# Cross-attention: the second half of the next tile's scores moved in among the transposes, and two probability chunks moved behind the masked copy

## The chip, the cores and the metric

The kernel runs on one core of one Trainium2 chip. Four engines compute: TensorE (PE in the profile; its weight loads are PEld), VectorE (DVE), ScalarE (ACT) and GpSimd (POOL). SyncE (SP) issues transfers. Each engine takes its instructions in order and waits on semaphores for the others. The metric is the time of one execution on the device, in microseconds (us).

## The reference

One decoder block over 2048 rows of width 256: self-attention, cross-attention onto 1601 context rows, and a layer with ternary weights. The change lies in the cross-attention:

```python
Q = q @ Wq.T + bq                     # q: layernorm(x), 2048 x 256
K = k @ Wk.T + bk                     # k, v: the context, 1601 x 256
V = v @ Wv.T + bv
e = jnp.einsum('bsd,btd->bst', Q, K) / jnp.sqrt(jnp.float32(d_k))
e = jnp.where(mask == 0, MASK_FILL, e)
a = jax.nn.softmax(e, axis=-1)
y = jnp.einsum('bst,btd->bsd', a, V)
return y @ Wo.T + bo                  # added to x
```

Everything is float32. The kernel keeps that precision by splitting an operand into a rounded high part and a low part (the difference), and multiplying the parts.

## The kernel before

The program goes through phases, each with its own block of instructions for each engine: self-attention, `fold` (it multiplies weights together so that queries meet the context directly, and values already carry the output weights), `cross`, and `feed` (the last layer). `cross` is the one that is changed. It takes the 2048 rows in 16 tiles of 128; the 1601 keys stand in 13 blocks of 128 (the last has 65), which make four `CHUNKS` of 4, 4, 4 and 1 blocks. Tiles 0 and 1 and tiles 14 and 15 are written out; tiles 2 to 13 are six turns of a hardware loop of two bodies. So there are 16 bodies, and all but the last also prepare the next tile.

For tile i, with h = i % 2 choosing the buffer:

- TensorE, `body` (L1398): `score(i+1, 0)`, the first half of the next tile's scores (12 matmuls of 512 columns into banks 0 and 1); then, once the exponentials of tile i are there (`exp_done`), the transposes of the 13 blocks of e into three banks `t_bank`, chunk by chunk. Chunk 3 goes into the bank of chunk 0, and so waits at L1406 until VectorE has read that bank (`p_low`). Then `score(i+1, 1)`, the second half of the scores (6 matmuls of 512 columns and 6 of 66, banks 2 and 3); then y, the probabilities times the values: two matmuls for each block, 26 in all, and each chunk waits for its own `p_low`.
- ScalarE, `body`: copies each chunk of transposes out of PSUM as the rounded high part of the probabilities (L1356, `p_high`), then takes the exponential of tile i+1 (L1346) when its row maximum is known.
- VectorE, `body` (L1289): for each chunk, the low part of the probabilities, `t_bank` minus the high part (L1295, `p_low`); then `take(i+1)` (L1263): it waits for all the scores of the next tile (`e_ready`) and copies them where the mask is set out of banks 0 to 3 into e (L1270, `e_taken`), reduces e to the row maximum (L1272) and scales that (L1274); then a normalization of the tile before and the addition of y to x (L1281 to L1322).
- GpSimd: when all transposes of tile i are done (`t_ready`), it fills e's buffer for tile i+2 with the row's mask value (L1239) and computes the low part of that tile's queries (L1231, `qc_low`), for which `score(i+2, 0)` waits. Then it does its part of the normalization.

So the order of the work is an order written out by hand for each engine. In the next tile's scores, a semaphore is raised only by the last matmul of the second half.

Of the kernel before, what the change touches and what calls it, by code (L numbers as in the profile page):

```python
# [1093 lines left out]
def cross(nc, ctx, io, keep, psum):  # L1094
# [32 lines left out]
    CHUNKS = [(c * TPB, min(TPB, S2_TILES - c * TPB)) for c in range(-(-S2_TILES // TPB))]  # L1127
# [42 lines left out]
    def keys_of(j):  # L1170
        return P if j < S2_TILES - 1 else S2_TAIL
# [11 lines left out]
    with nc.Block() as block:  # L1183
# [76 lines left out]

        @block.vector
        def _(dve):
            def take(i, h):  # L1263

                dve.wait_ge(mask_loaded[h], (i - h) * 8 + 16)
                dve.wait_ge(filled, i + 1)
                dve.wait_ge(e_ready, i + 1)

                dve.sem_inc(waits_met, 1)
                nc.vector.copy_predicated(e[:, h, :], mask[:, h, :], e_bank[:, 0:S2]).then_inc(e_taken, 1)  # L1270
                dve.wait_ge(e_taken, i + 1)
                nc.vector.tensor_reduce(neg[:, h:h + 1], e[:, h, :], axis=AX_X, op=ALU.max).then_inc(max_done, 1)  # L1272
                dve.wait_ge(max_done, 2 * i + 1)
                nc.vector.tensor_scalar(neg[:, h:h + 1], neg[:, h:h + 1], -X_SCALE, None,  # L1274
                                        ALU.mult).then_inc(max_done, 1)

            def scale_row(i):
                dve.wait_ge(pool_step, i * POOL_STEPS + POOL_STEPS)
                if not isinstance(i, int) or i:
                    dve.wait_ge(zg_done, i)  # L1280
                nc.vector.tensor_scalar(z[:, :], x[:, i, :], mv[:, 0:1], scale[:, :],  # L1281
                                        ALU.subtract, ALU.mult).then_inc(z_done, 1)

            def largest(i):
                dve.wait_ge(xn3_done, i + 1)
                nc.vector.tensor_reduce(abs_max[:, bass.ds(i, 1)], x3[:, i, :], axis=AX_X, op=ALU.max,
                                        apply_absolute_value=True).then_inc(abs_done, 1)

            def body(i, h, last):  # L1289

                for n, (j, m) in enumerate(CHUNKS):
                    rows = P if n < NCH - 1 else S2_TAIL
                    dve.wait_ge(y_ready, i)
                    dve.wait_ge(p_high, i * NCH + n + 1)
                    nc.vector.tensor_tensor(p_parts[1][0:rows, j:j + m, :].rearrange("p j q -> p (j q)"),  # L1295
                                            t_bank[n % 3][0:rows, 0:m * P],
                                            p_parts[0][0:rows, j:j + m, :].rearrange("p j q -> p (j q)").bitcast(F32),
                                            ALU.subtract).then_inc(p_low, 1)
                if not last:
                    take(i + 1, 1 - h)  # L1300
                if not isinstance(i, int) or i >= 1:
                    scale_row(i - 1)
                if not isinstance(i, int) or i >= 2:
                    largest(i - 2)

                dve.wait_ge(exp_done, i + 1)
                nc.vector.reciprocal(rsum[:, h:h + 1], esum[:, h:h + 1]).then_inc(rsum_done, 1)
                dve.wait_ge(rsum_done, i + 1)
                dve.wait_ge(y_ready, i + 1)
                nc.vector.scalar_tensor_tensor(out=x[:, i, :], in0=y_bank[:, 0:E], scalar=rsum[:, h:h + 1],  # L1310
                                               in1=x[:, i, :], op0=ALU.mult, op1=ALU.add).then_inc(half_added, 1)
                dve.wait_ge(half_added, i + 1)
                nc.vector.scalar_tensor_tensor(out=x[:, i, :], in0=y_bank[:, E:2 * E], scalar=rsum[:, h:h + 1],
                                               in1=x[:, i, :], op0=ALU.mult, op1=ALU.add).then_inc(x_added, 1)
                dve.wait_ge(x_added, i + 1)
                dve.sem_inc(waits_met, 1)
                nc.vector.bn_stats(out=stats[:, :], in_=x[:, i, :]).then_inc(stats_done, 1)
                dve.wait_ge(stats_done, i + 1)
                dve.wait_ge(pool_step, i * POOL_STEPS)

                dve.sem_inc(waits_met, 1)
                nc.vector.bn_aggr(out=mv[:, :], in_=stats[:, :]).then_inc(mv_done, 1)  # L1322
            take(0, 0)
            for n, tiles in enumerate(V_JOBS):
                rows, m = keys_of(tiles[-1]), len(tiles)
                dve.wait_ge(v_high, n + 1)
                nc.vector.tensor_tensor(v_parts[0:rows, tiles[0]:tiles[0] + m, 1, :],
                                        v_bank[n % 2][0:rows, 0:m * E].rearrange("p (m e) -> p m e", m=m),
                                        v_parts[0:rows, tiles[0]:tiles[0] + m, 0, :].bitcast(F32),
                                        ALU.subtract).then_inc(v_low, 1)  # L1330
            pairs(dve, body)
            scale_row(TILES - 1)
            largest(TILES - 2)
            largest(TILES - 1)
# [46 lines left out]
        def _(pe):  # L1381
            def score(i, h, part):

                if part == 0:
                    pe.wait_ge(e_taken, i)
                    pe.wait_ge(qc_low, i + 1)
                starts = list(range(0, S2, BLK))
                for c0 in (starts[:2], starts[2:])[part]:
                    c1 = min(c0 + BLK, S2_EVEN)
                    products = [(k, *pieces) for k in range(EC) for pieces in ((0, 0), (0, 1), (1, 0))]  # L1390
                    for k, left, right in products:
                        last = nc.tensor.matmul(e_bank[:, c0:c1], qc_parts[left][:, h, k, :],  # L1392
                                                ctx_parts[right][:, k, c0:c1], start=(k, left, right) == products[0],
                                                stop=(k, left, right) == products[-1])
                if part == 1:
                    last.then_inc(e_ready, 1)

            def body(i, h, last):  # L1398
                if not last:
                    score(i + 1, 1 - h, 0)  # L1400

                pe.wait_ge(exp_done, i + 1)
                for n, (j0, m) in enumerate(CHUNKS):
                    if n == 3:

                        pe.wait_ge(p_low, i * NCH + 1)  # L1406
                    for j in range(j0, j0 + m):
                        keys = P if j < S2_TILES - 1 else S2_TAIL
                        last_t = nc.tensor.transpose(t_bank[n % 3][0:keys, (j - j0) * P:(j - j0 + 1) * P],  # L1409
                                                     e[:, h, j * P:j * P + keys], ident[:, :])  # L1410
                    last_t.then_inc(t_ready, 1)
                if not last:
                    score(i + 1, 1 - h, 1)

                pe.wait_ge(x_added, i)
                for n, (j0, m) in enumerate(CHUNKS):
                    pe.wait_ge(p_low, i * NCH + n + 1)
                    for j in range(j0, j0 + m):
                        keys = P if j < S2_TILES - 1 else S2_TAIL
                        end = j == S2_TILES - 1  # L1420
                        for part in ((0, 1), (1, 0))[end]:
                            cols = y_bank[:, 0:E] if part else y_bank[:, :]
                            values = v_parts[0:keys, j, 0, :] if part else \
                                v_parts[0:keys, j, :, :].rearrange("p n e -> p (n e)")
                            mm = nc.tensor.matmul(cols, p_parts[part][0:keys, j, :], values,  # L1425
                                                  start=j == 0 and part == 0, stop=end and part == 0)
                mm.then_inc(y_ready, 1)
# [3 lines left out]
            for n, tiles in enumerate(V_JOBS):  # L1431
# [3 lines left out]
                for m, j in enumerate(tiles):  # L1435
                    for k in range(EC):
                        last = nc.tensor.matmul(v_bank[n % 2][0:keys_of(j), m * E:(m + 1) * E],
                                                ctx_t[:, k, j * P:j * P + keys_of(j)], w_vo[:, k, :],
                                                start=k == 0, stop=k == EC - 1)
# [237 lines left out]
```

## Time and profile before

| | |
|---|---|
| median of 3 runs | 847.97 us (847.71 to 848.97) |
| the profiled execution | 847.01 us, of which the span from first to last instruction is 844.9 us |
| busy in the span | PE 760.4 us (90%), DVE 613.6 (73%), ACT 423.6 (50%), POOL 168.1 (20%) |
| first transposes of tile 0 to first transposes of tile 15 | 629.66 to 803.07 us |

A busy PE is not PE at its peak, since its matmuls overlap; distances between starts tell more. Times in the rows are us from the start of the span.

### The profile page before, as it was taken

Reading aid. Unit: us, or ns where it says so; the run is one execution under the profiler, and the core shown is the slowest. Engines: PE = TensorE matmul, PEld = TensorE weight load, DVE = VectorE, ACT = ScalarE, POOL = GpSimd, SP = SyncE. Lnnn points to the kernel's source line nnn. Section 1 sums busy time; section 2 is a strip of 40 time slices with the busy share of each in tenths; the row PEclk is TensorE's granted clock in tenths of the full one; section 3 lists DMA queues with packets and bytes.
Section 4 is the critical chain, followed back from the end, with each engine's and each line's share of the span. In section 5 each row is a group of like instructions: output and inputs, shape, how many; then the busy total and the mean of one; then the engine's idle time right before and its main releaser. Section 6 shows DMA issues by size and latency. Waiting matters only on the chain. (4 is left out here: it accounts for less than half of the span.)

```text
span 844.9 us, 12146 instructions
## 1 busy us (share of the span) xinstructions
PE 760.4 (90%) x4265; PEld 394.8 (47%) x4265; DVE 613.6 (73%) x1106; ACT 423.6 (50%) x871; POOL 168.1 (20%) x236
## 2 busy tenths in 40 slices
PE   8864888999999999999999979898689999999857
PEld 5441322333232332223333312785468888888746
DVE  5899687889988899998887620476046777777734
ACT  1552553776577766567778769221233323332331
POOL 2663000000000000000000000032405556655430
PEclk9996896999999999999999989999999999999988
DMA  7795411200000000000800000300012211222002
GB/s 212 214 271 170 103 51 38 64 26 26 2 1 2 2 1 2 1 1 14 278 2 1 1 2 1 110 1 0 1 39 79 78 55 61 78 78 78 1 0 100
DMA packets 27088, 47.32 MB, mean 56 GB/s; under 512 B 6048, under 2 KB 22944, under 8 KB 26272
## 3 DMA queue, kind: packets, MB, share of 16 engines
q1 hardware_dynamic: 25120, 43.94, 17.2%
q10 hardware_dynamic: 1920, 2.75, 1.1%
q8 instruction: 29, 0.48, 0.2%
q14 instruction: 19, 0.16, 0.1%
HBM read 38.16 MB, written 8.39 MB: 55 GB/s over the span
## 5 line engine op out<-in xcount | busy, mean ns | idle before, releaser
L486 DVE TENSOR_REDUCE part_max<-psum 128x1 f32<-128x512 f32 (+3 forms) x560 | 341.3, 668 | 54.6 <-PE psum L672 49.5
L591 ACT ACTIVATE probs<-psum 128x512 f32<-128x512 f32 (+3 forms) x640 | 293.7, 540 | 154.8 <-PE psum L697 153.8
L672 PE MATMUL psum<-k_stack,q_stack 96*128 96x512 bf16 (+4 forms) x640 | 214.8, 364 | 18.8 <-DVE psum L472 11.5
L697 PE MATMUL psum<-q_stack,k_stack 98*128 98x512 bf16 (+4 forms) x640 | 202.2, 357 | 13.1 <-DMA q_stack<-shift 11.3
L709 PE MATMUL psum<-probs,v_all 128*17 128x512 f32 (+3 forms) x1280 | 149.2, 538 | 0.3 <-PE psum L683 0.2
L672 PEld LDWEIGHTS psum<-k_stack,q_stack 96*128 96x128 bf16 (+1 forms) x640 | 60.1, 99 | 171.7 <-DVE part_max L486 121.0
L697 PEld LDWEIGHTS psum<-q_stack,k_stack 98*128 98x128 bf16 (+1 forms) x640 | 60.8, 99 | 94.2 <-ACT probs L591 39.2
L877 POOL MEMSET eps<- 128x4 f32 x1 | 0.1, 101 | 458.8 <-POOLq L273 458.8
L1392 PE MATMUL psum<-ctx_part,qc_part 128*128 128x512 f32 (+1 forms) x384 | 84.7, 371 | 5.0 <-POOL qc_part L1231 4.1
L1425 PE MATMUL psum<-v_parts,p_part 128*128 128x512 f32 (+3 forms) x416 | 76.8, 341 | 0.0
L1392 PEld LDWEIGHTS psum<-ctx_part,qc_part 128*128 128x128 f32 x384 | 67.3, 192 | 18.8 <-issue 4.9
L1346 ACT ACTIVATE e<-e,neg 128x1601 f32<-128x1601 f32 x16 | 26.2, 1636 | 90.0 <-DVE neg L1274 83.9
L1425 PEld LDWEIGHTS psum<-v_parts,p_part 128*128 128x128 f32 (+1 forms) x416 | 63.7, 188 | 8.4
L1270 DVE COPY_PREDICATED e<-mask,psum 128x1601 f32<-128x1601 int32 x16 | 33.1, 2069 | 37.7 <-PE psum L1392 24.4
L1295 DVE TENSOR_TENSOR p_part<-psum,p_part 128x512 fp32r<-128x512 f32 x64 | 33.3, 582 | 23.3 <-ACT p_part L1356 23.3
L1239 POOL TENSOR_TENSOR e<-zeros_s,row_fill 128x1601 f32<-128x1601 f32 x16 | 45.6, 2852 | 21.7 <-PE psum L1409 20.3
L1356 ACT ACTIVATE p_part<-psum 128x512 fp32r<-128x512 f32 x64 | 29.6, 517 | 30.2 <-PE psum L1409 30.2
L709 PEld LDWEIGHTS psum<-probs,v_all 128*17 128x17 f32 x1280 | 21.4, 95 | 49.4 <-ACT probs L591 36.7
L1409 PE MATMUL psum<-ident,e 128*128 128x128 f32 (+1 forms) x208 | 28.8, 277 | 10.8 <-DVE p_part L1295 9.2
L1409 PEld LDWEIGHTS psum<-ident,e 128*128 128x128 f32 (+1 forms) x208 | 24.0, 140 | 17.0 <-DVE p_part L1295 13.0
L509 DVE RECIPROCAL rsum<-psum 128x16 f32<-128x16 f32 x16 | 4.1, 254 | 37.9 <-PE psum L683 37.4
L1272 DVE TENSOR_REDUCE neg<-e 128x1 f32<-128x1601 f32 x16 | 29.1, 1821 | 0.6
(135 smaller groups left out, 674.6 us busy)
## 6 DMA issues: line engine op xcount, KB each, us to landing
mask<-in_mask SPq DMA_DIRECT2D x16, 800.5 KB, 4.3
pieces<-k_stack SPq DMA_DIRECT2D x24, 256.0 KB, 4.9
q_stack<-pieces SPq DMA_DIRECT2D x24, 256.0 KB, 4.2
k_stack<-pieces SPq DMA_DIRECT2D x24, 256.0 KB, 4.7
x_sb<-in_x SPq DMA_DIRECT2D x4, 512.0 KB, 8.8
out<-y SPq DMA_DIRECT2D x4, 512.0 KB, 2.9
q_stack<-in_ctxT SPq DMA_DIRECT2D x1, 1601.0 KB, 10.8
probs<-in_cos ACTq DMA_DIRECT2D x4, 256.0 KB
```

What stands on the lines that cost most here:

```text
L486: nc.vector.tensor_reduce(part_max[:, h:h + m, r, c:c + 1], src, axis=AX_X, op=ALU.max).then_inc(m_read, 1)
L591: nc.scalar.activation(probs[:, s % 2, h, col:BLK], s_bank[h][:, col:BLK], ACT.Exp, scale=ATTN_SCALE).then_inc(exp_done, 1)
L672: last = nc.tensor.matmul(out, q_stack[b][0:rows, g * G + h, r * P:(r + 1) * P], k_stack[c][0:rows, g * G + h, 0:keys], start=True, stop=True)
L697: nc.tensor.matmul(s_bank[h][:, col:BLK], k_stack[s // TPB][0:rows, g * G + h, (s % TPB) * P:(s % TPB + 1) * P], q_stack[b][0:rows, g * G ...
L709: last = nc.tensor.matmul(o_bank[32 * h:32 * h + VW, col:BLK], v_all[:, s, g * G + h, :], probs[:, s % 2, h, col:BLK], start=s == 0, stop= ...
L1239: nc.gpsimd.tensor_tensor(e[:, h, :], zeros[:, :], value.to_broadcast([P, S2]), ALU.add).then_inc(filled, 1)
L1270: nc.vector.copy_predicated(e[:, h, :], mask[:, h, :], e_bank[:, 0:S2]).then_inc(e_taken, 1)
L1295: nc.vector.tensor_tensor(p_parts[1][0:rows, j:j + m, :].rearrange("p j q -> p (j q)"), t_bank[n % 3][0:rows, 0:m * P], p_parts[0][0:rows, ...
L1356: nc.scalar.activation(p_parts[0][0:rows, j:j + m, :].rearrange("p j q -> p (j q)"), t_bank[n % 3][0:rows, 0:m * P], ACT.Copy).then_inc(p_ ...
L1392: last = nc.tensor.matmul(e_bank[:, c0:c1], qc_parts[left][:, h, k, :], ctx_parts[right][:, k, c0:c1], start=(k, left, right) == products[ ...
L1409: last_t = nc.tensor.transpose(t_bank[n % 3][0:keys, (j - j0) * P:(j - j0 + 1) * P], e[:, h, j * P:j * P + keys], ident[:, :])
L1425: mm = nc.tensor.matmul(cols, p_parts[part][0:keys, j, :], values, start=j == 0 and part == 0, stop=end and part == 0)
```

## The change

On TensorE, `score(i+1, 1)` now stands ahead of chunk 2 of the transposes, which is between the eighth and the ninth transpose, and no longer behind the thirteenth. On VectorE, the low parts of chunks 2 and 3 are computed behind the masked copy of the next tile and ahead of its reduction, and no longer ahead of the copy. The last tile, which has no next one, keeps its order. No operation is added or taken away.

```diff
-            def take(i, h):
+            def take(i, h, between=lambda: None):
...
                 nc.vector.copy_predicated(e[:, h, :], mask[:, h, :], e_bank[:, 0:S2]).then_inc(e_taken, 1)
+                between()
                 dve.wait_ge(e_taken, i + 1)
                 nc.vector.tensor_reduce(neg[:, h:h + 1], e[:, h, :], axis=AX_X, op=ALU.max).then_inc(max_done, 1)
...
-                for n, (j, m) in enumerate(CHUNKS):
+                def rest_of_probs(n):
+                    j, m = CHUNKS[n]
                     rows = P if n < NCH - 1 else S2_TAIL
...
-                if not last:
-                    take(i + 1, 1 - h)
+                def second_half():
+                    rest_of_probs(2)
+                    rest_of_probs(3)
+
+                rest_of_probs(0)
+                rest_of_probs(1)
+                if last:
+                    second_half()
+                else:
+                    take(i + 1, 1 - h, second_half)
...
                 for n, (j0, m) in enumerate(CHUNKS):
+                    if n == 2 and not last:
+                        score(i + 1, 1 - h, 1)
                     if n == 3:
...
-                if not last:
-                    score(i + 1, 1 - h, 1)
```

On TensorE, one body of the loop, from the first transpose to the first matmul of y, stood before as follows (L1409 are transposes, L1392 scores, L1425 y; `ident` is the identity matrix, `p_part` the high or low probabilities):

```order
L1409 MATMUL psum<-ident,e 128x128 [waits exp_done3]
L1409 MATMUL psum<-ident,e 128x128 x11
L1406 ISA
L1409 MATMUL psum<-ident,e 65x128 [waits p_low]
L1392 MATMUL psum<-ctx_part,qc_part 128x512 x6
L1392 MATMUL psum<-ctx_part,qc_part 128x66 x6
L1425 MATMUL psum<-v_parts,p_part 128x512 [waits p_low,x_added3]
```

And now, where the lines have moved down by ten or twelve:

```order
L1421 MATMUL psum<-ident,e 128x128 [waits exp_done3]
L1421 MATMUL psum<-ident,e 128x128 x7
L1402 MATMUL psum<-ctx_part,qc_part 128x512 x6
L1402 MATMUL psum<-ctx_part,qc_part 128x66 x6
L1421 MATMUL psum<-ident,e 128x128 x4
L1418 ISA
L1421 MATMUL psum<-ident,e 65x128 [waits p_low]
L1435 MATMUL psum<-v_parts,p_part 128x512 [waits p_low,x_added3]
```

The twelve score matmuls have moved ahead of four transposes and of the transpose that waits for VectorE; the last five transposes now stand right ahead of y.

On VectorE, the same body stood before as follows, from the second low part to the reduction:

```order
L1295 TENSOR_TENSOR p_part<-psum,p_part 128x512 [waits p_high]
L1294 REGISTER_ALU [waits y_ready3]
L1295 TENSOR_TENSOR p_part<-psum,p_part 128x512 [waits p_high]
L1294 REGISTER_ALU [waits y_ready3]
L1295 TENSOR_TENSOR p_part<-psum,p_part 65x128 [waits p_high]
L1265 ISA
L1266 REGISTER_ALU [waits mask_loaded1]
L1270 COPY_PREDICATED e<-mask,psum 128x1601 [waits filled,e_ready]
L1272 TENSOR_REDUCE neg<-e 128x1 [waits e_taken]
```

And now:

```order
L1297 TENSOR_TENSOR p_part<-psum,p_part 128x512 [waits p_high]
L1265 ISA
L1266 REGISTER_ALU [waits mask_loaded1]
L1270 COPY_PREDICATED e<-mask,psum 128x1601 [waits filled,e_ready]
L1296 REGISTER_ALU [waits y_ready3]
L1297 TENSOR_TENSOR p_part<-psum,p_part 128x512 [waits p_high]
L1296 REGISTER_ALU [waits y_ready3]
L1297 TENSOR_TENSOR p_part<-psum,p_part 65x128 [waits p_high]
L1273 TENSOR_REDUCE neg<-e 128x1 [waits e_taken]
```

The low parts of chunks 2 and 3 have moved from ahead of the copy to behind it, so that they stand behind its wait for the next tile's scores.

## Rows read from the trace of the kernel before

**Rows 1.** Stretches: busy of each engine (instructions), granted clock, DMA share, GB/s

```profile
640.00:664.00 24.00, 22.79 (x130) 19.34 (x129) 16.91 (x29) 8.37 (x17) 14.11 (x22) 1.00 0.21 71
...
815.00:819.00 4.00, 1.97 (x8) 1.57 (x8) 1.05 (x3) 0.63 (x2) 1.44 (x2) 0.56 0.00 0
...
827.00:831.00 4.00, 4.00 (x15) 3.30 (x15) 1.60 (x4) 0.00 (x0) 0.00 (x0) 0.73 0.00 0
```

**Rows 2.** PE in time, a loop tile: start, length, work [idle before, releaser]

```profile
664.76 1.48 PE L1409 MATMUL psum<-ident,e 128*128 128x128 f32 x12
666.78 0.32 PE L1409 MATMUL psum<-ident,e 128*65 128x128 f32 x1 [0.54 <-DVE p_part L1295]
666.86 2.24 PE L1392 MATMUL psum<-ctx_part,qc_part 128*128 128x512 f32 x12
668.93 4.81 PE L1425 MATMUL psum<-v_parts,p_part 128*128 128x512 f32 x26
673.58 2.96 PE L1392 MATMUL psum<-ctx_part,qc_part 128*128 128x512 f32 x12
676.38 1.47 PE L1409 MATMUL psum<-ident,e 128*128 128x128 f32 x12
```

**Rows 3.** Who waited for whom, 640 to 800 us: total, times, longest

```profile
PEld psum L1409 <- DVE p_part L1295: 11.2, 14, 0.9
PE psum L1409 <- DVE p_part L1295: 7.8, 14, 0.7
```

**Rows 4.** PE in time, tile 0 and tile 14 (written-out bodies)

```profile
629.66 1.48 PE L1409 MATMUL psum<-ident,e 128*128 128x128 f32 x12
631.81 0.33 PE L1409 MATMUL psum<-ident,e 128*65 128x128 f32 x1 [0.68 <-DVE p_part L1295]
...
792.37 1.47 PE L1409 MATMUL psum<-ident,e 128*128 128x128 f32 x12
...
794.61 2.24 PE L1392 MATMUL psum<-ctx_part,qc_part 128*128 128x512 f32 x12
...
803.07 1.53 PE L1409 MATMUL psum<-ident,e 128*128 128x128 f32 x12 [1.58 <-ACT e L1346]
```

**Rows 5.** DVE in time, the loop tile of rows 2

```profile
666.03 0.69 DVE L1295 TENSOR_TENSOR p_part<-psum,p_part 128x512 fp32r<-128x512 f32 x1 [1.18 <-ACT p_part L1356]
...
667.24 0.88 DVE L1295 TENSOR_TENSOR p_part<-psum,p_part 128x512 fp32r<-128x512 f32 x2
...
669.24 2.07 DVE L1270 COPY_PREDICATED e<-mask,psum 128x1601 f32<-128x1601 int32 x1 [1.12 <-issue]
671.34 1.82 DVE L1272 TENSOR_REDUCE neg<-e 128x1 f32<-128x1601 f32 x1
```

**Rows 6.** Weight loads for y and the next scores, rows 2's tile

```profile
668.90 0.19 PEld L1425 LDWEIGHTS psum<-v_parts,p_part 128*128 128x128 f32 x1
...
671.71 0.19 PEld L1425 LDWEIGHTS psum<-v_parts,p_part 128*128 128x128 f32 x1
...
673.35 0.19 PEld L1392 LDWEIGHTS psum<-ctx_part,qc_part 128*128 128x128 f32 x1
```

**Rows 7.** ACT in time, the same tile

```profile
665.40 1.57 ACT L1356 ACTIVATE p_part<-psum 128x512 fp32r<-128x512 f32 x3 [1.60 <-PE psum L1409]
...
674.93 0.18 ACT L1346 ACTIVATION_READ_ACCUMULATOR e<-e,neg 128x1 f32 x1
```

**Rows 8.** POOL in time, the same tile

```profile
667.40 2.85 POOL L1239 TENSOR_TENSOR e<-zeros_s,row_fill 128x1601 f32<-128x1601 f32 x1
670.21 0.74 POOL L1231 TENSOR_TENSOR qc_part<-x_t,qc_part 128x256 fp32r<-128x256 f32 x1
```

**Rows 9.** Minimum, median and longest ns, first transposes of tile 1 to tile 14: fill, masked copy

```profile
L1239 POOL TENSOR_TENSOR e<-zeros_s,row_fill x13: 2851/2852/2854, 644.0 to 783.4; 128x1601 f32<-128x1601 f32 x13
...
L1270 DVE COPY_PREDICATED e<-mask,psum x13: 2061/2077/2079, 646.1 to 785.2; 128x1601 f32<-128x1601 int32 x13
```

**Rows 10.** DVE in time, tile 14: its masked copy

```profile
797.10 2.06 DVE L1270 COPY_PREDICATED e<-mask,psum 128x1601 f32<-128x1601 int32 x1 [1.24 <-PE psum L1392]
```

## Prediction

> **What bounds the kernel now.** I read first the stretches by engine, which tell how full each engine is in the phase that is changed. In the cross-attention TensorE is busy 22.8 us of 24 with the clock granted in full, VectorE 16.9, GpSimd 14.1 and ScalarE 8.4 [rows 1]. So TensorE is the candidate, and the question is what ends its idle time. The list of waits has one entry for it in the steady part: the transposes of L1409 wait for VectorE's low parts of L1295, 14 times, at most 0.7 us on PE and 0.9 on its weight loads [rows 3]. Then I read PE's rows in time for one tile and measured from start to start. Call T the first transpose, 664.76. The twelve transposes of chunks 0 to 2 start from T on; the thirteenth starts at T+2.02; the second half of the scores at T+2.10, y at T+4.17, the next first half at T+8.82, the next transposes at T+11.62 [rows 2]. All of that is back to back but for the thirteenth transpose. It writes into the bank of chunk 0, which VectorE reads until 666.03 + 0.69 = 666.72, and it starts 0.06 later [rows 2, 5]. So a tile costs 11.62, TensorE's own work plus this one wait. The exponential is no limit there: its last part ends at 675.11, T+10.35, and the next transposes come at T+11.62 [rows 2, 7].
>
> **What the change removes.** A transpose takes one pitch of (1.48 - 0.27)/11 = 0.11, with 0.27 as the length of one alone (an estimate: 0.32 is that of the thirteenth) [rows 2]. Without a wait the thirteenth would start 12 x 0.11 = 1.32 after the first; it starts at 2.02, so 0.70 goes. The scores follow it only 0.08 later, and a thirteenth in a stream would be followed after 0.11, so 0.03 is given back: 0.67 for a tile. In the new order the wait asks for nothing late: the low part of chunk 0 is there at T+1.96, and the thirteenth transpose now comes at 8 x 0.11 + 2.07 (scores to y, 666.86 to 668.93) + 4 x 0.11 = T+3.39 [rows 2, 5].
>
> **The sum.** Tiles 2 to 13 run in the loop: 12 x 0.67 = 8.0. Tiles 0 and 1 are written out, and there the thirteenth transpose comes 631.81 - 629.66 = 2.15 after the first: 0.13 more each, so 0.80, twice: 1.6 [rows 4]. Tile 14 is followed by a tile for which no first half of scores is left to compute, so its end is set by the exponential (1.58 idle, released by ACT) [rows 4]. There the gain is what VectorE's chain wins. The score half starts 0.88 after the first transpose and not 794.61 - 792.37 = 2.24, so 1.36 earlier, but two low parts worth 0.88 now stand ahead of the reduction [rows 4, 5]: 0.5. Tile 15 has no next tile, and keeps its order: 0. Together 10.1 us. The profiled execution took 847.01, which gives 836.9; the median of the runs stands 0.96 above that execution, so that I expect **837.9**.
>
> **What is hidden, and by how much.** Nothing is added, but four things come closer to being late. The times are from T in the new order, in which y's first matmul stands at 3.39 + 0.11 = 3.50, its first weight load at 3.47, and the next transposes at 11.62 - 0.67 = 10.95.
>
> First, chunk 2 of y. Its weight load comes 671.71 - 668.90 = 2.81 after y's first, so at T+6.28 [rows 6]. It needs the low part of chunk 2, which now stands behind the masked copy. The copy starts 669.24 - 666.86 = 2.38 after the score half, at 3.26, and takes 2.07: 5.33 [rows 2, 5]. The next VectorE instruction follows 0.03 later (671.31 to 671.34), takes 0.69, and 0.06 passes to TensorE: 6.11. The margin is 0.17 us. In the written-out bodies the copy starts 797.10 - 794.61 = 2.49 after the scores, which leaves 0.06 [rows 4, 10]. This is the thinnest place. Behind a late low part stand the rest of y, y's addition and the next scores, so that all lateness is paid in full. ScalarE's part for chunk 2 is not the limit: its transposes start at 2.95 to 3.28, and a copy follows the first four transposes of a tile by 665.40 - 664.76 = 0.64 and takes some 0.6, so it is done near 4.2, under the masked copy [rows 2, 7].
>
> Second, GpSimd. Its fill for tile i+2 waits for the thirteenth transpose. It started 667.40 - 666.78 = 0.62 after it (in part because GpSimd was still busy), now at 3.39 + 0.62 = 4.01; the low query follows 2.81 later and takes 0.74: 7.56 [rows 2, 8]. The weight load of the next first half comes 673.35 - 668.90 = 4.45 after y's first, at 7.92 [rows 6]. The margin is 0.36, where it was 673.35 - 670.95 = 2.40.
>
> Third, the next exponential. The two low parts end at 5.36 + 0.88 = 6.24, and the reduction, which started at T+6.58, starts 0.34 earlier than it did [rows 5]. So the exponential ends at 10.35 - 0.34 = 10.0, against transposes at 10.95: the ring through VectorE and ScalarE is not the bound.
>
> Fourth, VectorE's sum of work is unchanged, 16.9 us of 24; a tile that is 0.67 shorter makes it some 75% busy [rows 1].
>
> **The rivals.**
>
> Late low part of chunk 2 (15 in 100). The copy now runs beside ScalarE's copies of chunks 2 and 3 and beside transposes into a third bank, where before it ran beside y alone. Against a stretch speaks that it keeps to 2061 to 2079 ns in all bodies [rows 9], and that the low part of chunk 0, which runs beside ScalarE's copies of chunks 1 and 2, takes 0.69, and those three copies 1.57 together [rows 5, 7]. The bounds for its lateness: nothing, or 0.6 us for one ScalarE copy in its way [rows 7], which is 0.43 past the margin. I take nothing, being nearest to the rows of the copy itself. At the upper end 15 bodies pay 0.43 = 6.5, and the time is 844.4; at 0.2 past the margin it is 840.9.
>
> The wait only changes its place (4 in 100). If the low part comes 0.17 + 0.67 = 0.84 late, TensorE stands in y as long as it stood in the transposes, and the time is 848. It would take a copy 40% longer than any row shows.
>
> GpSimd's low query is late: slower (4 in 100). The fill and the low query move by some 1.4 us and now lie under VectorE's reduction of e, which the rows of before never have under the fill: the fill ran 667.40 to 670.25, the reduction from 671.34 [rows 5, 8]. If one of the two kept the other out of the memory, the fill would end up to 1.82 later, the low query would be there at 9.38 and TensorE 1.46 late, in the 14 bodies that prepare a tile after next: 14 x 1.46 = 20 lost against 10 won, 858. It decides for slower once the stretch is over 0.36 + 0.67 = 1.03. Against it: the fill does run under the low parts and the masked copy, and takes 2851 to 2854 ns in every tile [rows 9]. The Trainium skill, "SBUF — State Buffer", section "Who interferes with whom", says that VectorE and GpSimd share one pair of ports as an exclusive lock, that a VectorE instruction with at most one SBUF input outside the two-port modes leaves it alone, and that a tensor_reduce on trn2 never contends; by that rule this rival doesn't come about, and where the trace has the two engines together it agrees, with 2851 to 2854 ns.
>
> The tail's clock. Behind the cross-attention the granted clock is 0.56 of full speed from 815 to 819 us, after TensorE had been idle for long, and 0.73 from 827 to 831, where it goes back to its full level [rows 1]. That part is only shifted, but where in the last matmuls the clock comes back can shift too: half of 4 us either way at most, so 2 us, in the forecast's own range.
>
> **How the numbers follow.** The forecast has 73 in 100, the late low part 15, the same place 4, GpSimd 4, and 4 are left for a gain that is larger or smaller for a reason that I don't see (say 3 of them faster, 1 slower or same). A measurement of this kernel can tell 0.2%, 1.7 us, from no change. Faster then is 0.73 + 0.15 + 0.03 = 0.91, within 0.2% 0.04, slower 0.05. The forecast's own range is 837.9 less 2 and plus 2; the range for 8 in 10 goes down to 835.9 and up to 842, which takes in the late low part up to 0.27 past its margin.
>
> **What would show it.** In the profile after: the idle time of the thirteenth transpose is gone and its start is 0.11 behind the twelfth; the first transposes of the loop's tiles stand 10.9 to 11.0 apart, not 11.6; the masked copy keeps 2.06 to 2.08; no matmul of y waits for L1297; the low query ends before y does; tile 15's transposes still wait for ACT. The prediction is wrong if the list of waits names y's matmuls waiting for VectorE, or the first half of the scores waiting for GpSimd, or if the distance of tiles stays over 11.3.

## The result, and the profile after

| | before | after |
|---|---|---|
| median | 847.84 us (847.63 to 848.97, 4 runs) | 836.92 us (836.77 to 837.19, 4 runs) |
| ratio | | 0.9869, 95% interval 0.9852 to 0.9886 |
| span of the profiled execution | 844.9 us | 834.7 us |

The forecast was 837.9 us, with a range of 835.9 to 842.0: right in sign, size and range. By the medians 10.9 us are gone; the spans of the two profiled executions, which the rows below come from, are 10.2 us apart.

First the stretch by engine that answers to [rows 1], from the profile after:

```profile
640.00:664.00 24.00, 24.00 (x142) 20.81 (x141) 17.04 (x30) 8.72 (x17) 15.10 (x25) 1.00 0.21 69
```

TensorE is busy for all of the 24 us, where it was for 22.79, and gets through 142 matmuls, not 130. Then PE in time, over one tile of the loop, as in [rows 2] (in this kernel L1421 are the transposes, L1402 the scores, L1435 y):

```profile
662.62 1.04 PE L1421 MATMUL psum<-ident,e 128*128 128x128 f32 x8
663.41 2.24 PE L1402 MATMUL psum<-ctx_part,qc_part 128*128 128x512 f32 x12
665.49 0.77 PE L1421 MATMUL psum<-ident,e 128*128 128x128 f32 x5
666.01 4.83 PE L1435 MATMUL psum<-v_parts,p_part 128*128 128x512 f32 x26
670.68 2.97 PE L1402 MATMUL psum<-ctx_part,qc_part 128*128 128x512 f32 x12
```

No idle time stands in brackets any more (the list of waits from 640 to 790 us names none of TensorE's at all), and the thirteenth transpose has merged with the four ahead of it into one group of five. From the first transpose T = 662.62 the score half starts at 0.79, the ninth transpose at 2.87, y at 3.39, the next first half at 8.06; the forecast had 0.88, 2.95, 3.50 and 8.15.

VectorE and ScalarE in the same tile, in answer to [rows 5] and [rows 7], and GpSimd, in answer to [rows 8]:

```profile
663.89 1.29 DVE L1297 TENSOR_TENSOR p_part<-psum,p_part 128x512 fp32r<-128x512 f32 x2 [1.07 <-ACT p_part L1366]
665.79 2.06 DVE L1270 COPY_PREDICATED e<-mask,psum 128x1601 f32<-128x1601 int32 x1 [0.61 <-PE psum L1402]
667.74 0.86 DVE L1297 TENSOR_TENSOR p_part<-psum,p_part 128x512 fp32r<-128x512 f32 x2
668.53 1.80 DVE L1273 TENSOR_REDUCE neg<-e 128x1 f32<-128x1601 f32 x1
```
```profile
666.18 0.76 ACT L1366 ACTIVATE p_part<-psum 128x512 fp32r<-128x512 f32 x2 [1.84 <-PE psum L1421]
...
672.09 0.18 ACT L1356 ACTIVATION_READ_ACCUMULATOR e<-e,neg 128x1 f32 x1
```
```profile
666.43 2.85 POOL L1239 TENSOR_TENSOR e<-zeros_s,row_fill 128x1601 f32<-128x1601 f32 x1 [1.02 <-PE psum L1421]
669.24 0.74 POOL L1231 TENSOR_TENSOR qc_part<-x_t,qc_part 128x256 fp32r<-128x256 f32 x1
```

The masked copy waits for the scores and then takes 2.06, with both of ScalarE's copies (666.18 to 666.94) under it. The two low parts stand behind it; the first of them starts 0.11 us ahead of the copy's end. The fill lies under the copy, the low parts and the reduction, and keeps to 2.85.

Now the whole phase, from PE in time: the first transposes of tile 0 and of tile 2, then tiles 14 and 15, the transposes of the normalized rows behind them (L1464), and the 64 matmuls of the last layer (L1575):

```profile
630.12 1.04 PE L1421 MATMUL psum<-ident,e 128*128 128x128 f32 x8
...
651.80 0.93 PE L1421 MATMUL psum<-ident,e 128*128 128x128 f32 x7
...
781.92 1.04 PE L1421 MATMUL psum<-ident,e 128*128 128x128 f32 x8
...
791.78 2.93 PE L1421 MATMUL psum<-ident,e 128*128 128x128 f32 x13 [1.67 <-ACT e L1356]
794.36 5.31 PE L1435 MATMUL psum<-v_parts,p_part 128*128 128x512 f32 x26
799.50 0.71 PE L1464 MATMUL psum<-ident,attn 128*128 128x128 f32 x5
...
813.45 16.98 PE L1575 MATMUL psum<-w_tern,xq_t 128*128 128x256 f32 x64 [2.55 <-DVE xq_t L1533]
```

Twelve tiles take 781.92 - 651.80 = 130.12, so 10.84 each, against (792.37 - 653.15)/12 = 11.60 before, where tile 2 starts at 653.15. From tile 0's transposes to those of tile 15 it is 161.66 us, against 803.07 - 629.66 = 173.41: 11.75 gained. Of that the span shows 10.2. The rest is 0.46 that this execution was later at tile 0, where nothing was changed, 0.75 in tile 15, and 0.34 behind it. The 0.34 lies in the last layer's matmuls, 16.98 and not 16.63: the granted clock comes back to its full level two of them later. The 0.75 is worth a look, because it came with the change. From tile 15's first transpose to the rows' transposes it is 799.50 - 791.78 = 7.72, where it was 810.04 - 803.07 = 6.97, as PE in time of the kernel before shows (first tile 2, last the last layer):

```profile
653.15 1.04 PE L1409 MATMUL psum<-ident,e 128*128 128x128 f32 x8
...
805.28 0.33 PE L1409 MATMUL psum<-ident,e 128*65 128x128 f32 x1 [0.68 <-DVE p_part L1295]
805.38 4.82 PE L1425 MATMUL psum<-v_parts,p_part 128*128 128x512 f32 x26
810.04 2.13 PE L1454 MATMUL psum<-ident,attn 128*128 128x128 f32 x18
...
823.97 16.63 PE L1565 MATMUL psum<-w_tern,xq_t 128*128 128x256 f32 x64 [2.55 <-DVE xq_t L1523]
```

The stretches of the two kernels over tile 15 tell why, after first, then before: the granted clock (third from the end) is 0.63 of full in the one, a mean over its two levels, and 1.00 in the other. From the third to the twelfth transpose of tile 15 the starts are 0.20 to 0.21 us apart, where at the full clock it is 0.11.

```profile
791.00:795.00 4.00, 3.22 (x15) 2.88 (x16) 2.62 (x6) 2.44 (x6) 2.64 (x8) 0.63 0.00 0
```
```profile
803.00:807.00 4.00, 3.25 (x22) 2.83 (x23) 3.07 (x8) 1.87 (x5) 2.20 (x8) 1.00 0.00 0
```

### The profile page after: what moved, and what is told of

The parts are those of the page before. It is cut to its first block and busy times, and to the rows that moved or that the text cites. A ratio compares the mean times of both kernels' runs of the same rounds, so it can differ in the third digit from the quotient of the medians.

```text
span 834.7 us, 12146 instructions
## 1 busy us (share of the span) xinstructions
PE 760.8 (91%) x4265; PEld 397.3 (48%) x4265; DVE 611.8 (73%) x1106; ACT 423.7 (51%) x871; POOL 168.5 (20%) x236
## 5 line engine op out<-in xcount | busy, mean ns | idle before, releaser
L1402 PE MATMUL psum<-ctx_part,qc_part 128*128 128x512 f32 (+1 forms) x384 | 84.6, 371 | 5.0 <-POOL qc_part L1231 4.1
L1435 PE MATMUL psum<-v_parts,p_part 128*128 128x512 f32 (+3 forms) x416 | 77.7, 343 | 0.0
L1402 PEld LDWEIGHTS psum<-ctx_part,qc_part 128*128 128x128 f32 x384 | 67.2, 192 | 18.8 <-issue 4.8
L1435 PEld LDWEIGHTS psum<-v_parts,p_part 128*128 128x128 f32 (+1 forms) x416 | 64.4, 190 | 8.6
L709 PEld LDWEIGHTS psum<-probs,v_all 128*17 128x17 f32 x1280 | 21.4, 95 | 49.4 <-ACT probs L591 36.7
L1421 PE MATMUL psum<-ident,e 128*128 128x128 f32 (+1 forms) x208 | 30.0, 285 | 1.7 <-ACT e L1356 1.7
L1011 PE MATMUL psum<-q_stack 128*128 128x256 f32 (+2 forms) x128 | 26.5, 358 | 0.0
## 6 DMA issues: line engine op xcount, KB each, us to landing
q_stack<-in_ctxT SPq DMA_DIRECT2D x1, 1601.0 KB, 10.9
```

What stands on the lines that cost most here:

```text
L709: last = nc.tensor.matmul(o_bank[32 * h:32 * h + VW, col:BLK], v_all[:, s, g * G + h, :], probs[:, s % 2, h, col:BLK], start=s == 0, stop= ...
```

## The experiments

Each ratio is to the kernel before on the same chip. That kernel had a median of 849.59 us beside the first four, 848.94 beside the three after them and 848.36 beside the last two, so ratios are compared, not times. Four of the experiments first: they take the two moves apart, shift the place of the split, and make the low parts late.

**TensorE's move alone.**

```diff
-                    take(i + 1, 1 - h, second_half)
+                    second_half()
+                    take(i + 1, 1 - h)
```

> TensorE's order of after, VectorE's order of before (all four low parts ahead of the masked copy). Theory (the two moves belong together: the wait goes by TensorE's move, but the low parts of chunks 2 and 3 now wait for late transposes and would hold up the masked copy): in the profile after, ScalarE's copy of chunk 2 starts 3.56 after a tile's first transpose and the low part follows 0.63 later, so the masked copy starts near T+5.1 and not at 3.2; the reduction starts 1.2 to 1.3 later than after, the exponential ends near T+10.9, and the next transposes wait for ScalarE some 0.3 a tile: tiles 11.15 apart, 842 us. Rival (VectorE has room enough, its move is worth nothing): 836.9, tiles 10.85 apart.

Measured: 841.5 us, ratio 0.9922 (0.9902 to 0.9942), slower than the changed kernel's 0.9869. From its profile, VectorE and the weight loads in time:

```profile
667.39 0.88 DVE L1297 TENSOR_TENSOR p_part<-psum,p_part 128x512 fp32r<-128x512 f32 x2 [1.62 <-ACT p_part L1367]
668.19 2.07 DVE L1270 COPY_PREDICATED e<-mask,psum 128x1601 f32<-128x1601 int32 x1
```
```profile
674.12 0.42 PEld L1422 LDWEIGHTS psum<-ident,e 128*128 128x128 f32 x4 [0.34 <-ACT e L1357]
```

VectorE idles 1.62 for ScalarE's copy of the late transposes; the masked copy starts 668.19 - 663.15 = 5.04 after the tile's first transpose (663.15) and not at 3.17, and the next transposes wait for the exponential, 4.9 us in 14 waits between 640 and 790 us. This tile takes 674.12 - 663.15 = 10.97, and the mean of the loop is 10.95. So the theory stands, and the price in the loop was set too high: 0.1 a tile over the changed kernel, not 0.3. TensorE's move brings 0.65 us of the 0.76 a tile by itself; VectorE's move is needed for the rest. The loop's 1.3 us are not all that is lost: tile 14, whose end hangs on VectorE, takes 794.76 - 783.62 = 11.14 and not 9.86, another 1.3, and tiles 0 and 1 take 0.5 more together. The profiled execution was the fastest of the five, 838.38 us, in part because its last layer took 15.49 and not 16.98.

**VectorE's move alone.**

```diff
-                    if n == 2 and not last:
-                        score(i + 1, 1 - h, 1)
...
+                if not last:
+                    score(i + 1, 1 - h, 1)
```

> VectorE's order of after, TensorE's order of before. Theory: the thirteenth transpose waits as before (start 2.0 after the first), the masked copy starts at T+4.5 as before, the low part of chunk 2 is there near 7.15, and the weight load of y's chunk 2 wanted it at 6.94: y pauses 0.2 a tile, tiles 11.8 apart, 851 us, slower than before. Rival (late low parts are absorbed in the weight loads that run ahead): 847.8, as before.

Measured: 853.43 us, ratio 1.0049 (1.0033 to 1.0064). PE in time, then the weight loads of its y:

```profile
670.84 0.32 PE L1419 MATMUL psum<-ident,e 128*65 128x128 f32 x1 [0.54 <-DVE p_part L1297]
670.92 2.24 PE L1402 MATMUL psum<-ctx_part,qc_part 128*128 128x512 f32 x12
672.99 5.01 PE L1435 MATMUL psum<-v_parts,p_part 128*128 128x512 f32 x26
```
```profile
675.98 1.70 PEld L1435 LDWEIGHTS psum<-v_parts,p_part 128*128 128x128 f32 x10 [0.27 <-DVE p_part L1297]
```

The old wait is there with its 0.54, and y has a second one, at its seventeenth weight load, for the low part that now stands behind the copy; y takes 5.01 and not 4.81. The loop's tiles are 11.82 apart, 0.2 more than before. Slower, as the theory had it.

**The split behind the twelfth transpose,** with three low parts ahead of the copy and one behind it.

```diff
-                    if n == 2 and not last:
+                    if n == 3 and not last:
...
                 def second_half():
-                    rest_of_probs(2)
                     rest_of_probs(3)
...
                 rest_of_probs(0)
                 rest_of_probs(1)
+                rest_of_probs(2)
```

> The score half stands behind the twelfth transpose and not behind the eighth, and only the low part of chunk 3 stands behind the masked copy. TensorE's work and its number of changes between kinds are the same. Theory (TensorE's stream alone sets the time once no wait is in it): 836.9 within 1 us, tiles 10.85 apart, though the masked copy starts 0.4 later and the low part of chunk 2 is there 3 us before it is wanted. Rival (some of the gain came from the earlier masked copy): slower than after by up to 0.4 a tile, 843.

Measured: 836.18 us, ratio 0.9853 (0.9834 to 0.9872), which overlaps the changed kernel's. PE in time, then VectorE:

```profile
664.67 2.23 PE L1402 MATMUL psum<-ctx_part,qc_part 128*128 128x512 f32 x12
666.73 0.30 PE L1421 MATMUL psum<-ident,e 128*65 128x128 f32 x1
666.79 4.81 PE L1435 MATMUL psum<-v_parts,p_part 128*128 128x512 f32 x26
671.44 2.97 PE L1402 MATMUL psum<-ctx_part,qc_part 128*128 128x512 f32 x12
674.25 1.48 PE L1421 MATMUL psum<-ident,e 128*128 128x128 f32 x12
```
```profile
664.71 1.89 DVE L1297 TENSOR_TENSOR p_part<-psum,p_part 128x512 fp32r<-128x512 f32 x3 [1.21 <-ACT p_part L1366]
667.04 2.08 DVE L1270 COPY_PREDICATED e<-mask,psum 128x1601 f32<-128x1601 int32 x1 [0.44 <-issue]
669.00 0.27 DVE L1297 TENSOR_TENSOR p_part<-psum,p_part 65x128 fp32r<-65x128 f32 x1
```

The starts of the loop's tiles are 10.81 apart. Counted from this tile's first transpose, 674.25 - 10.81 = 663.44, the masked copy starts at 3.60, 0.43 later than in the changed kernel. Chunk 2's low part is done at 666.60, where the copy has not started yet. Nothing of that makes it slower: what counts is that TensorE has no wait. Where the split stands is worth at most 0.04 a tile, 10.81 against 10.84, which came the same in three profiles of either order.

**The low parts behind the reduction.**

```diff
                 nc.vector.copy_predicated(e[:, h, :], mask[:, h, :], e_bank[:, 0:S2]).then_inc(e_taken, 1)
-                between()
...
                                         ALU.mult).then_inc(max_done, 1)
+                between()
```

> As after, but the low parts of chunks 2 and 3 stand behind the reduction and its scaling, 1.95 later than in after. Theory (lateness at y's chunk 2 past its margin is paid in full): after has the low part at T+5.79 and the weight load at 6.19, a margin of 0.35; so TensorE waits 1.6 to 1.7 in y of each of 15 tiles, tiles 12.5 apart, 861 to 862 us. Rival (the wait overlaps with other slack, such as the earlier exponential): below 850.

Measured: 862.77 us, ratio 1.0166 (1.0144 to 1.0187). PE in time:

```profile
672.07 3.06 PE L1435 MATMUL psum<-v_parts,p_part 128*128 128x512 f32 x16
676.64 2.02 PE L1435 MATMUL psum<-v_parts,p_part 128*128 128x512 f32 x10 [1.51 <-DVE p_part L1297]
```

After 16 matmuls of y, which are chunks 0 and 1, TensorE stands for 1.51. The tiles are about 12.6 apart, 1.8 more than in the changed kernel. The lateness is paid in every tile and in full; the rival that the earlier exponential makes up for it is out.

**GpSimd later,** by an operation ahead of each fill whose result is not used.

```diff
+                    nc.gpsimd.tensor_tensor(spare[:, :], zeros[:, 0:800], zeros[:, 0:800], ALU.add)
                     fill(i + 2, h)
                     lower_query(i + 2, h)
```

> As after, with one additional GpSimd operation of 800 columns (half a fill, some 1.4 us, its result is not used) ahead of each fill of bodies 0 to 13. Theory (the slower rival of the prediction has the right price and a margin of 0.43 in after: low query ends at T+7.36, weight load at 7.83): TensorE waits 1.0 us for the low query in 14 bodies, tiles 11.85 apart, 850 to 851 us. Rival (GpSimd's lateness is taken up elsewhere): 837 to 840.

Measured: 848.88 us, ratio 0.9996 (0.9986 to 1.0006). GpSimd in time, then PE:

```profile
669.16 1.52 POOL L1248 TENSOR_TENSOR spare<-zeros_s 128x800 f32<-128x800 f32 x1 [1.36 <-PE psum L1423]
670.64 2.85 POOL L1240 TENSOR_TENSOR e<-zeros_s,row_fill 128x1601 f32<-128x1601 f32 x1
673.45 0.73 POOL L1232 TENSOR_TENSOR qc_part<-x_t,qc_part 128x256 fp32r<-128x256 f32 x1
```
```profile
674.24 3.08 PE L1404 MATMUL psum<-ctx_part,qc_part 128*128 128x512 f32 x12 [0.56 <-POOL qc_part L1232]
677.15 1.03 PE L1423 MATMUL psum<-ident,e 128*128 128x128 f32 x8
```

With 1.5 us more on GpSimd, TensorE waits for it in each tile and the whole gain is gone; tiles are 11.7 apart (665.45 to 677.15), 0.84 more than in the changed kernel. The theory is right in kind and was 0.2 a tile too dear.

**Tile 15 and the tail.** In two runs TensorE is given matmuls whose result is not used. In the first, seven of 512 columns stand in tile 15's wait for the exponential:

```diff
+                else:
+                    pe.wait_ge(e_taken, TILES)
+                    keep_busy(e_bank[:, 0:BLK], 7)
```

> As after, with seven additional matmuls of 512 columns (their result is not used) put into the 1.8 us in which TensorE waits for the exponential of tile 15. Theory (after that idle time the granted clock fell in tile 15, 0.68 from 791 to 794 us, and its transposes went at 0.21 and not 0.11 us, which took back 0.7 to 0.8 of the gain): the clock stays at 1.00, tile 15's transposes are 0.11 apart, and the time is 0.7 to 0.8 lower, 836.1. Rival (the fall has nothing to do with the idle time): transposes of tile 15 still 0.21 apart, 836.9 or, by the matmuls, a little more.

Measured: 835.84 us, ratio 0.9846 (0.9829 to 0.9863). PE in time and one stretch:

```profile
792.85 1.53 PE L1428 MATMUL psum<-ident,e 128*128 128x128 f32 x12
795.05 0.32 PE L1428 MATMUL psum<-ident,e 128*65 128x128 f32 x1 [0.68 <-DVE p_part L1297]
795.15 4.83 PE L1442 MATMUL psum<-v_parts,p_part 128*128 128x512 f32 x26
799.82 2.78 PE L1471 MATMUL psum<-ident,attn 128*128 128x128 f32 x24
```
```profile
790.00:794.00 4.00, 3.94 (x25) 3.15 (x25) 3.26 (x9) 2.12 (x3) 1.67 (x3) 1.00 0.00 0
```

The clock stays at 1.00, and tile 15 takes 799.82 - 792.85 = 6.97, as before the change: the 0.75 is back in the profile. The ratio's interval overlaps the changed kernel's, so the timing alone does not show it. Nor does this run show that the idle time decides: with GpSimd later, TensorE stood 1.69 us at this place without any such matmuls, and the clock stayed at 1.00 and tile 15 took 6.95.

In the second, the order of the split behind the twelfth transpose has those seven, and more of them in the later waits (16 ahead of the last eight transposes of the normalized rows, 3 ahead of the maximum's transpose, 9 ahead of the last layer):

```diff
+                if tb == NB - 1:
+                    keep_busy(banks(psum, 7), 16)
                 pe.wait_ge(xn3_done, (tb + 1) * TPB)
...
+            keep_busy(banks(psum, 4), 3)
             pe.wait_ge(top_done, 1)
...
+            keep_busy(banks(psum, 4), 9)
             for tb in range(NB):
```

> The order of e3_split12 (score half behind the twelfth transpose, three low parts ahead of the masked copy), with unused matmuls in tile 15's wait (7) and in the later waits of TensorE (16 ahead of the last eight transposes of the normalized rows, 3 ahead of the maximum's transpose, 9 ahead of the last layer). Theory (the tail runs at the lower clock only because TensorE idles there): the last eight transposes take 1.0 and not 2.0 us, the 64 matmuls of the last layer start at the full clock, which saves 1.7 to 2.5; together 3 to 4 us below e3, 832.5. Rival (the tail is set by VectorE, ScalarE and GpSimd, and the matmuls only stand in the way): within 1 us of e3, or over it.

Measured: 834.32 us, ratio 0.9822 (0.9801 to 0.9844), the fastest median of this study. By the ratios that is 0.3%, 2.6 us, below the split alone, less than was expected, and the intervals overlap. PE in time of the last layer's 64 matmuls, with the additional ones, then of the split alone:

```profile
811.22 3.87 PE L1575 MATMUL psum<-ctx_part 128*128 128x512 f32 x9
814.88 14.08 PE L1591 MATMUL psum<-w_tern,xq_t 128*128 128x256 f32 x64
```
```profile
812.07 16.52 PE L1575 MATMUL psum<-w_tern,xq_t 128*128 128x256 f32 x64 [2.55 <-DVE xq_t L1533]
```

The 64 matmuls take 2.4 us less, but they start later: 21.4 after tile 15's first transpose (814.88 - 793.50) and not 20.0 (812.07 - 792.04), because the nine, with the granted clock at 0.71 in 810 to 814 us, stood in the way. The last eight transposes of the rows had nothing to give: they take 1.09, and took 1.14 in the split alone, not the 2.0 that was expected of it. So the last layer does run faster behind a busy TensorE, as the theory had it, and the matmuls in front of it take back about half of that, as the rival had it.

**The changed kernel again, beside the split with the busy wait.** Both are given above; no other edit was made.

> The changed kernel once more, unaltered, to stand on one chip with the next run. Expected: as measured, a ratio of 0.987 to the kernel before. If the fall of the clock in tile 15 belongs to this kernel and not to one execution, tile 15's transposes are 0.21 us apart again.

> The order of e3_split12 with the seven unused matmuls in tile 15's wait. Theory (e3 is after with wider margins; its tiles are 10.81 and not 10.85 apart and tile 15's wait ends 0.14 earlier; tile 15 keeps the clock): 14 x 0.035 + 0.14 + 0.75 = 1.4 us below after. Rival (it is the same within the measurement, the tiles' pitch being TensorE's own in both): less than 0.5 below.

Measured: 837.6 us, ratio 0.9863 (0.9828 to 0.9899), for the changed kernel again, and 835.2 us, 0.9838 (0.9805 to 0.9872), for the split. The intervals overlap, so whether the split is faster by 1.4 us or the same stays open. (The split's profiled execution was its slowest, 842.25 us; 8 us of that lie ahead of tile 0, where nothing was changed.) The fall of the clock did come again in the changed kernel, where tile 15 takes 7.73 and its transposes are 0.21 apart from the sixth on; in the split with the busy wait tile 15 takes 6.97. The stretch of the changed kernel:

```profile
791.00:797.00 6.00, 4.75 (x22) 4.22 (x23) 4.67 (x13) 3.15 (x6) 3.62 (x10) 0.72 0.00 1
```

## Why the prediction was right

**The bound.** It named TensorE's stream with one wait in it. The profile after has no wait in the loop and a stream of 10.84 a tile; the split at another place gives the same time within the intervals; and each run that puts a wait back into the stream (low parts behind the reduction, GpSimd later) pays for it. That is shown.

**The removed wait.** The forecast was 0.67 a tile for the loop; measured is 11.60 - 10.84 = 0.76. The term was sized too small by 0.09, and the rows after say where. The prediction assumed that a long matmul follows a transpose after one pitch, 0.11. It follows sooner: the score half starts at 663.41, and the eighth transpose started at 662.62 + 7 x 0.11 = 663.39, so the distance is 0.02 to 0.03; y stands as close behind the thirteenth transpose. That is 0.08 less than assumed, at two places. (The long matmul after that one starts 0.32 later and not 0.23, in both kernels; this lies within the 2.07 and the 4.65 that the forecast took from the rows, and does not count again.) Of these 0.16 us, 0.06 goes back at the ninth transpose, which stands behind short score matmuls: the next one follows it only after 0.17 (665.49 + 0.77 - 0.27 - 3 x 0.11 = 665.66 is its start). In 12 tiles the gain is 9.1, not 8.0.

**Tiles 0, 1 and 14.** The forecast was 1.6 for the first two and 0.5 for tile 14. The first two gained (653.15 - 629.66) - (651.80 - 630.12) = 1.81, the same 0.1 a tile over the forecast. Tile 14 gained (803.07 - 792.37) - (791.78 - 781.92) = 0.84. The step that was off there is the price of two low parts ahead of the reduction, 0.88: behind a copy for whose result they don't wait, the first starts 0.11 before its end, and the reduction starts 0.68 after that end (668.53 - 667.85), where it stood at 0.03 behind it. The two low parts cost 0.65. Most of what is left is the score half, which starts 0.80 and not 0.88 after tile 14's first transpose.

**What was to be hidden.** The low part of chunk 2 was forecast for T+6.11 with a weight load at 6.28. It ends at 667.74 + 0.67 = 668.41, T+5.79, and the weight load comes at T+6.19. With the 0.06 that the forecast allowed for the way to TensorE, the margin is 0.34, not 0.17, mostly for the reason just given. That a late one is paid in full is shown by the run with the low parts behind the reduction, and by the run with VectorE's move alone. The low query was forecast for T+7.56 and ends at 669.98, T+7.36; the scores' weight load comes at 670.45, T+7.83, so 0.47 is left, not 0.36. That lateness here is paid too is shown by the run with GpSimd later. The exponential ends at 672.27, T+9.65, against a forecast of 10.0.

**The rivals.** The masked copy is not stretched by ScalarE's copies under it: 2.06. The slower rival, GpSimd and VectorE keeping each other out of the memory, did not come about: with the reduction over the last part of the fill (668.53 on, the fill ending at 669.28), the fill takes 2.85. The Trainium skill, "SBUF — State Buffer", section "Who interferes with whom", has a tensor_reduce never contend on trn2; the trace agrees, with those 2.85 us. The kind of loss that this rival feared is real, though: 1.5 us more on GpSimd takes back all of the gain. Its size was set somewhat high, since past the margin of 0.47 some 1.05 of the 1.52 is left, and a tile became 0.84 longer.

**What it missed.** Tile 15 was put at nothing, because its order is the same. In fact the granted clock falls there after TensorE's wait for the exponential (1.67 idle), to a mean of 0.63, and that costs 0.75. Behind tile 15 the prediction did allow for a shift of the place where the clock comes back, up to 2 us either way; it came out at 0.34. Why the clock fell in tile 15 stays open. It fell in both profiles of the changed kernel (1.67 and 1.69 idle) and in that of TensorE's move alone (2.87 idle, 0.69 from 797 to 800 us). It stayed at 1.00 before (1.58), with the split behind the twelfth transpose (1.57), with GpSimd later (1.69) and with VectorE's move alone (1.91), and in the three runs whose wait was filled. So the length of the idle time does not decide it alone: after 1.69 it fell in one kernel and not in another, and after 1.91 it did not fall.

So the sum of 10.1 came out near the 10.2 of the spans partly by luck, by two errors that cancel: 11.75 in the tiles for the forecast's 10.1, and 1.55 given back, of which 0.46 is scatter between two executions, 0.75 lies in tile 15 and 0.34 behind it.

## What to carry to other kernels

When one wait interrupts an otherwise full engine, put independent work of that engine in front of the wait, and measure from start to start what it costs. Then look at the other engines: move back what now stands ahead of the work that the moved part makes possible earlier. TensorE's move alone was worth 0.8%, both together 1.3%, VectorE's alone was a loss of 0.5%. For each engine behind the moved step write down the margin until somebody waits for it, since lateness past it is paid in every tile. Two orders with the same stream were the same within the measurement here, though their margins differ. Look once at the clock behind the place, too: in two profiles of the changed kernel it fell after a short idle time at the end of the phase, and slowed what followed.

## What the runs showed of the hardware

A long matmul (512 columns) starts 0.02 to 0.03 us after the transpose ahead of it, though transposes among themselves start 0.11 apart; the long one after it then starts 0.32 later and not 0.23, so that the two together take no less than their pitches. A VectorE operation that needs nothing from the one ahead started 0.11 us before that one's end; one that waits for it started 0.03 after it. On GpSimd an operation of 800 columns took 1.52 us where one of 1601 took 2.85. The granted clock fell to its lower level in tile 15 after 1.67 and 1.69 us of idle time in two executions of the changed kernel, and stayed at 1.00 after 1.57, 1.58, 1.69 and 1.91 in four other kernels.
